# Prologue of a recommendation kernel: weights and lookups load ahead of the indices, ScalarE takes over the copies of the turned weights, the indices are turned behind them

## The reference

```python
x = _mlp(dense_x, bot, sigmoid_last=False)
pooled = jax.vmap(lambda tab, ix: jnp.take(tab, ix, axis=0).sum(axis=1))(tables, indices)
Tcat = jnp.concatenate([x[:, None, :], jnp.transpose(pooled, (1, 0, 2))], axis=1)
Z = jnp.einsum('bim,bjm->bij', Tcat, Tcat)
R = jnp.concatenate([x, Z[:, li, lj]], axis=1)
return _mlp(R, top, sigmoid_last=True)
```

## Time and profile before

| what | value |
|---|---|
| median of 3 runs | 2874.72 us (2874.49 to 2882.71) |
| the profiled execution | 2880.54 us |
| its span in the trace | 2878.7 us |
| mean granted TensorE clock | 0.96 |
| busy: TensorE, its weight loads | 2756.6 us (96%), 1309.0 us |
| busy: VectorE, ScalarE, GpSimd | 1995.2, 2113.8, 1805.9 us |
| DMA traffic | 167.99 MB, mean 58 GB/s |

### The profile page before, as it was taken

How to read it: one execution, slowest core, us unless ns; L and a number is a source line. 1 busy time by engine, 2 the same in 40 slices (tenths; PEclk the granted TensorE clock), 3 DMA queues, 4 the chain that set the end, 5 groups by cost and what they waited for, 6 DMA issues and landing times.

```text
span 2878.7 us, 65596 instructions
## 1 busy us (share of the span) xinstructions
PE 2756.6 (96%) x24204; PEld 1309.0 (45%) x24204; DVE 1995.2 (69%) x3358; ACT 2113.8 (73%) x2496; POOL 1805.9 (63%) x1640
## 2 busy tenths in 40 slices
PE   5999999999999999999999999999999999999798
PEld 2344444444444444444444444444444444448574
DVE  4477787877878778787777877778777778734121
ACT  2678878788787787877878878788787887853232
POOL 3277777777777777777777777777777777200000
PEclk8999999999999999999999999999999999996668
DMA  2112122121221212212122121121221212118611
GB/s 69 62 32 76 31 76 74 32 76 30 76 74 32 76 29 77 75 30 76 42 64 76 31 78 55 49 77 29 78 73 33 76 29 76 31 29 129 119 31 31
DMA packets 173102, 167.99 MB, mean 58 GB/s; under 512 B 116104, under 2 KB 134328, under 8 KB 167476
## 3 DMA queue, kind: packets, MB, share of 16 engines
q1 hardware_dynamic: 121380, 110.94, 13.8%
q0 software_dynamic: 51200, 52.53, 8.0%
q10 hardware_dynamic: 272, 0.52, 0.1%
HBM read 143.83 MB, written 20.05 MB: 57 GB/s over the span
## 4 chain that ended last, share of the span: by engine, by line
PE 82%; ACT 11%; issue 3%; SPq 1%; DMA 1%; ACTq 1%; DVE 1%; DVEq 0%; POOL 0%; POOLq 0%
PE ps L693 58%; PE ps L674 14%; ACT counts L841 6%; PE ps L637 5%; PE ps L766 4%; ACT parts L803 4%; ACT parts L810 1%; SPq L509 0%; ACT h_bot L854 0%; DMA pooled<-pooled_sb 0%; ACTq L838 0%; SPq L532 0%; DMA look_in<-in_r_indices 0%; DMA products<-zt 0%; SPq L516 0%
## 5 line engine op out<-in xcount | busy, mean ns | idle before, releaser
L611 POOL DMA_INDIRECT rows<-in_L_rec_tables,look x1600 | 1788.8, 1118 | 622.9 <-issue 453.1
L841 ACT CAST counts<-ps 128x792 int32<-128x792 f32 (+1 forms) x1848 | 1712.3, 984 | 476.2 <-PE ps L674 463.5
L693 PE MATMUL ps<-counts,parts 128*128 128x512 fp8e3 x8232 | 2024.3, 389 | 0.0
L693 PEld LDWEIGHTS ps<-counts,parts 128*128 128x128 f16 x8232 | 719.2, 96 | 914.8 <-issue 11.5
L1058 DVE TENSOR_TENSOR onehot_p<-iota_by_unit,place 128x1024 bf16<-128x1024 bf16 x924 | 638.5, 691 | 395.4 <-PE ps L674 367.3
L674 PEld LDWEIGHTS ps<-onehot_c,onehot_p 60*128 60x128 bf16 x14448 | 370.5, 95 | 482.3 <-ACT counts L841 276.3
L674 PE MATMUL ps<-onehot_c,onehot_p 60*128 60x99 bf16 x14448 | 522.7, 208 | 56.1 <-ACT counts L841 39.2
L1063 DVE TENSOR_TENSOR onehot_c<-column_c,weighted_s 128x792 bf16<-128x792 bf16 x924 | 521.4, 564 | 0.0
L1019 DVE SCALAR_TENSOR_TENSOR raw<-raw,coef_next,parts 128x896 f32<-128x896 f32 x147 | 169.1, 1150 | 59.7 <-ACT parts L803 59.7
L1092 DVE TENSOR_REDUCE rows<-rows 128x64 f32<-128x384 f32 (+1 forms) x240 | 189.9, 791 | 13.9 <-DVE pooled_sb L1069 13.9
L394 DVE COPY zt<-ps 32x208 f32<-32x208 f32 x128 | 64.8, 507 | 151.0 <-PE ps L766 149.1
(11 more groups left out here) (82 smaller groups left out, 529.3 us busy)
## 6 DMA issues: line engine op xcount, KB each, us to landing
raw<-in_L_rec_tables SPq DMA_DIRECT2D x21, 1792.0 KB
raw<-in_L_rec_tables SPq DMA_DIRECT2D x21, 1344.0 KB
rows<-in_L_rec_tables,look POOLq DMA_INDIRECT x1600
pooled<-pooled_sb SPq DMA_DIRECT2D x84, 128.0 KB
slots<-pooled SPq DMA_DIRECT2D x30, 352.0 KB, 7.9
products<-zt SPq DMA_DIRECT2D x16, 351.0 KB
idx_raw<-in_r_indices SPq DMA_DIRECT2D x42, 79.7 KB
gathered<-bags_t SPq DMA_DIRECT2D x42, 64.0 KB
```

What stands on the lines that cost most here:

```text
L611: nc.gpsimd.indirect_dma_start(rows[:, s, l, :], None, rows_flat, bass.IndirectOffsetOnAxis(ap=look[:, c, s * PL + l:s * PL + l + 1].bitca ...
L693: mm = nc.tensor.matmul(acc[k % 2][:, 0:NB], parts[:, j, :], count_bytes[k % 2][:, j % COLS, 0:NB, j // COLS], start=(j == 0), stop=(j == ...
L841: nc.scalar.copy(counts[k % 2][:, :, u * UG * GS:(u * UG + g) * GS].rearrange("p c (g h s) -> p h g c s", h=HALVES, s=HS), unit_ps[unit_bu ...
```

## The change

- SyncE issues the first four of the weight loads (`xr`, `w_bot0r`, `w_bot1r`, `w_bot2r`) and the lookups before it waits for `const_step` 4. Then come the indices of table 0, the first table, the small top loads and, as before, the indices of table 1.
- The three loads of the biases are issued by ScalarE, as the first thing in its program.
- TensorE turns the weights first, as soon as `ident` is there and all seven weight loads have landed, and turns the indices of table 0 behind them.
- ScalarE copies the turned pieces out, one copy for each group of up to four transposes: eight copies take the place of VectorE's 30. It converts the indices only after the last of them.
- VectorE no longer copies the turned weights; its program goes from `make_lookup` straight to `max_chunk`.

Nothing is changed in what is computed, in the loop or in the last stage.

```diff
@@ SyncE @@
-            sp.wait_ge(const_step, 4)
-            load_indices(0)
             with nc.allow_non_contiguous_dma(reason="small weights and biases"):
-                for dst, src in weight_loads:
+                for dst, src in weight_loads[:4]:
                     sp.dma_start(dst, src).then_inc(weights_in, 16)
+                load_lookups(0)
+                sp.wait_ge(const_step, 4)
+                load_indices(0)
                 for h in range(2):
                     load_table(rows_flat[0:SPAN * P, :], h)
                 for dst, src in small_top_loads:
                     sp.dma_start(dst, src).then_inc(top_in, 16)
-            load_lookups(0)
             sp.wait_ge(idx_turned, 1)
             load_indices(1)
@@ TensorE @@
             pe.wait_ge(consts_ready, 1)
-            turn_indices(0, first=True)
             pe.wait_ge(weights_in, 16 * len(weight_loads))
             turn(pe, turns, turned, unturned)
+            turn_indices(0, first=True)
@@ ScalarE @@
+            with nc.allow_non_contiguous_dma(reason="biases"):
+                for dst, src in weight_loads[4:]:
+                    act.dma_start(dst, src).then_inc(weights_in, 16)
+            unturned_groups = [xT[:, i * 4 * P:(i + 1) * 4 * P].rearrange("p (k c) -> p k c", c=P)
+                               for i in range(B // P // 4)]
+            unturned_groups.append(w_bot0T[:, :].rearrange("p (k c) -> p k c", c=P))
+            unturned_groups += [w_bot1T[:, :, m * P:(m + 1) * P] for m in range(NBOT[2] // P)]
+            unturned_groups.append(w_bot2T[:, :, :])
+            for i, dst in enumerate(unturned_groups):
+                act.wait_ge(turned, i + 1)
+                m, items, kp = dst.shape
+                nc.scalar.copy(dst, banks[i % 4][0:m, 0:items * P].rearrange("p (k c) -> p k c", c=P)[:, :, 0:kp]
+                               ).then_inc(unturned, 1)
             convert_indices(0)
@@ VectorE @@
                 make_lookup(0, c, first=True)
-            unturn(dve, turns, turned, unturned)
             for q in range(CHUNKS):
                 max_chunk(0, q, first=True)
```

## The result

| | before | after |
|---|---|---|
| median | 2875.66 us (4 runs, 2874.49 to 2882.71) | 2855.36 us (4 runs, 2852.84 to 2857.25) |
| the profiled execution | 2880.54 us | 2852.84 us |
| its span | 2878.7 us | 2851.0 us |
| mean granted TensorE clock | 0.96 | 0.965 |

The changed kernel is 20.3 us faster, a ratio of 0.9924 with an interval of 0.9905 to 0.9942. Forecast were 15.1 us and 2859.6, with a range of 2853.5 to 2867.5 that holds the result.

The account below looks back on a forecast made before the run. TensorE bounds the loop, so gain must come from the first 120 us, where VectorE's copies wait for the lookups. Network at 17.8 instead of 32.93 gives -15.1 us, from median 2874.72 to 2859.6, range 2853.5 to 2867.5.

Parts of the forecast that it names:

- Loads of the weights cost nothing: Prologue: all seven weight loads are there at 7.6 at the latest, before `ident` at 9.17, a cover of 1.6 us.
- the rival of the late start: Start of the loads: SyncE's first DMA not before about 7.8, all 5.2 us later, 2864.8 us; chance 0.16.
- Turning to 16.1: Prologue: TensorE's weight transposes from 9.17 to 15.7, with ScalarE's eight copies beside them ending at 16.1.
- the cheap end of that term: Turning of the weights: transposes at full clock and copies of 0.42 us, done at 14.8.
- Indices 0.93+0.81: Prologue, behind the copies: index conversion 0.93 us and index transposes 0.81 us, so the network starts at 17.8.
- VectorE 9.7 earlier, 5.4 behind TensorE, slack of 7.3 enough: VectorE's maxima: start at 23.1 instead of 32.80; slack of 8.8 and 7.3 us covers the lag, 1.9 spare.
- The network keeps its length of 86.6: Bottom network: it starts 15.1 us earlier and still takes 86.6 us, with the clock's pattern kept.
- The rival of the faster clock: Network's start at full clock: first 13 passes 4.2 us shorter, only 1.9 kept, 2857.7 us; chance 0.12.
- Slower or eaten: Network at half clock throughout, 18 to 35 us more, chance 0.05; or 7 to 14 us come back, chance 0.12.
- The forecast's -15.1: Prologue: the whole predicted gain, from TensorE starting the network at 17.8 instead of 32.93.
- the lower edge of the range, 2853.5: Whole kernel: lowest time of the range, taken as cheap turning together with the faster clock.

Follow-up runs that it names:

- e10_dve_late: The changed kernel with five extra, unused chunk maxima on VectorE ahead of the seven; 2862.9 us (kernel before on the same chip 2878.2).
- b_again: The kernel before, run and profiled once more without an edit; 2873.84 us, ratio to its like 1.0.
- e6_idx_first: The changed kernel with the indices converted and turned ahead of the weights, as before; 2860.0 us (kernel before on the same chip 2878.2).
- e3b_dve_no_wait: The changed kernel with VectorE's copies, not ScalarE's, ahead of its index work and its wait for GpSimd's last constant; 2859.67 us (kernel before 2878.2).
- e11_delayed: The changed kernel with an extra unused fill on GpSimd (14.24 us) ahead of its first pattern; 2868.72 us (kernel before on the same chip 2873.9).
- e1_again: The changed kernel once more without an edit; 2855.36 us against 2878.2 for the kernel before, ratio 0.9926.
- e9_both: The changed kernel with GpSimd making ident and the idx_raw fill ahead of its patterns, plus an extra early reduction over partitions; 2856.2 us, ratio 0.9923.
- e5_biases_sp: The changed kernel with the biases issued by SyncE behind the four weights instead of by ScalarE; 2852.70 us, ratio 0.9921.
- e3_dve_copies: The changed kernel with VectorE's 30 copies put back ahead of its index work and none on ScalarE; 2861.0 us (kernel before 2878.2).
- e2_act_copies: The kernel before with only the copies of turned weights moved from VectorE to ScalarE, behind its index conversion; 2867.1 us, ratio 0.9953.
- e4_lookups_first: The kernel before with only the lookups' DMA moved, issued ahead of the first table instead of behind it; 2868.4 us, ratio 0.9969.
- e12_early_store: The changed kernel with the network's output stored in two parts, the first three blocks early by SyncE; 2852.16 us, ratio 0.9915.

## Why the prediction was right, and where it missed

The mechanism is the forecast one: the prologue was bound by VectorE standing at the lookups with TensorE's banks full, and with the reordering the bottom network starts as early as `ident`, the turns and the indices let it.

- **Loads of the weights cost nothing:** right, also with the biases on SyncE, and the fourth was issued at 3.81, so the rival of the late start did not occur. But `ident` came at 10.0 instead of 9.17.
- **Turning to 16.1:** came at 15.58 in spite of the later start. The transposes of `w_bot1` ran at the quick rate (8 in 1.04 us, which is the earlier trace rows), so the cheap end of that term was the true one. A grouped copy of 512 columns took 0.57 us, between the 0.42 and 0.69 of the rows used.
- **Indices 0.93+0.81:** 0.83+0.49. Together the network started at 16.8, not 17.8: 16.1 us earlier instead of 15.1.
- **VectorE 9.7 earlier, 5.4 behind TensorE, slack of 7.3 enough:** right in kind, and near the edge. It was 10.8 earlier, TensorE reached its first unit 17.6 earlier, so VectorE was 6.8 behind, and 0.5 of the slack was left where I forecast 1.9. e10_dve_late shows that a delay beyond it is waited for.
- **The network keeps its length of 86.6:** this step failed, and it is the term that was mis-sized. It took 85.2 (16.9 to 102.07). The first eight passes went from 6.19 us to 4.58. The length follows the time that TensorE spent at half clock between the network's first pass and its last (all us, b_again's first 13 counted as half, as they have no clock record but passes 0.85 apart, against 0.43 later):

| half clock in the network | length of the network | kernels |
|---|---|---|
| 24 | 83.6 | e6_idx_first |
| 27 | 85.0, 85.1 | e3b_dve_no_wait, e11_delayed |
| 31 | 85.0 to 85.4, 86.2 | changed, e1_again, e9_both, e5_biases_sp; e3_dve_copies |
| 34 | 86.6, 87.4 | before, e2_act_copies |
| 37 | 88.4, 89.1 | b_again, e4_lookups_first |

Left out are e10_dve_late and e12_early_store, where a wait or the store differs. The two ends of the table in the windows (line 637; length, busy and count of PE and PEld, clock, DMA share, GB/s), e6_idx_first and then e4_lookups_first:

```profile
20.55:97.70 77.15, 62.87 (x112) 21.24 (x112) 0.85 0.06 12
25.54:108.40 82.86, 69.05 (x112) 22.95 (x112) 0.77 0.07 11
```

So what failed is that the sum kept the clock's pattern of the kernel before. The kernel before alone came out at 86.6 and 88.4, so the size of the 1.4 us is partly luck. Still, all variants of the changed kernel in this table lie below both. Idle time ahead of the network does not order them: e6_idx_first and e2_act_copies have equally little. What decides where the clock falls is open. The rival of the faster clock was thus partly true, 1.4 us of its 4.2. The Trainium skill ("TensorE: Matmul & The Clock Gate", "What's actually happening") has activity lift the slow clock and idle time bring it back. The trace agrees only in part: behind 1.45 us of idle time the first eight passes took 4.58 us, behind 1.99 they had taken 6.19, but the second layer took 9.32 us after and 9.29 before, partly at half clock in both, though TensorE had stood only 0.78 us ahead of it.
- **Slower or eaten:** the clock did not stay at half. Over the network the granted clock was 0.81 after against 0.79.

The line-637 stretches of the changed kernel (length, busy and count of PE and PEld, clock, DMA share, GB/s):

```profile
16.80:21.50 4.70, 4.63 (x8) 1.26 (x8) 0.82 0.97 354
...
16.80:27.80 11.00, 10.20 (x16) 3.68 (x17) 0.69 0.52 169
...
16.80:97.00 80.20, 66.31 (x112) 21.77 (x112) 0.81 0.12 32
```

In the first 11 us there are 16 passes at 0.69 where the earlier trace rows had 13 at 0.55.

The forecast's -15.1 became -17.5 in the prologue, 1.0 of it by an earlier start and 1.4 by a shorter network. The other 3 of the medians' 20.3 fit in the spread of the kernel before: its second profile had a prologue longer by 2.3 us, and its loop varies by 1.5 us for each short stretch. That the forecast range holds the result owes something to this: the mechanism is the forecast one, but 5.2 us of the gain were not forecast. And the lower edge of the range, 2853.5, does not come out of its own terms: cheap turning (1.3 us) and the faster clock (1.9 that can be kept, 4.2 in all) give 2856.4 or 2854.1.

## What to carry to other kernels

A copy out of PSUM belongs on an engine that waits for nothing else at that point: here VectorE held four banks through an unrelated wait for a DMA queued behind 3 MB, and either of two single edits, another engine or another place in the queue, took back about half of it. Freed of its waits, VectorE was within 0.7 us of ScalarE (e3b_dve_no_wait). When a cover has been moved, look at what is left of the other engines' slack, for it is spent at once: 7.3 us had become 0.5. And before a difference of two profiles is explained, compare a stretch that the change does not touch: here it differed by 9.4 us of 27.7.

## What the runs showed of the hardware

- A short half-clock stretch in a loop at full clock is drawn anew in each run. It came 0 to 8 times in 20 tables, at about 1.5 us each, and only behind gaps of TensorE of 1.7 us or more (43 of 103 such gaps; behind none of 177 shorter ones).
- These stretches alone do not explain the spread of the kernel before. On one chip its executions lie between 2867.3 and 2885.1 us and hardly follow their mean granted clock (correlation -0.2 to -0.5 on three chips, against -0.8 to -1.0 in six of the other kernels).
- The 112 passes of the bottom network took 77.2 us with 24 us at half clock (e6_idx_first) and 82.9 with 37 (e4_lookups_first).
- GpSimd's first instruction other than a fill came 6.8 to 7.2 us after its configuration instruction (at 1.0) in kernels that issue no loads meanwhile, and 7.2 to 7.65 in eight that do (8.0 in e9_both, where the select comes first). This argues for the loads slowing it, at some 0.6 us, but was not tried by itself. In e11_delayed, with a fill of 14 us ahead and the loads long over, it was 6.81.
- GpSimd's first reduction over partitions started 5.6 to 5.8 us after its configuration instruction (29.7 to 35.39 in the changed kernel), 6.6 in e9_both, and later ones at once. The Trainium skill ("GPSIMD Engine Reference", "Instruction dispatch") gives some 6 us for the first call of a freshly loaded kernel without an instruction of its own in the profile, and the trace agrees within 0.7 us. An extra reduction takes it ahead (e9_both), which paid nothing here.
